# Row-wise inverse norms by VectorE transposes, with new orders on four engines, in a two-layer graph kernel

## The reference

```python
# layer 0: y = x mixed over the nodes with adj * adj, plus bias
x = layernorm(x + einsum('bnf,nm->bmf', x, adj * adj) + bias)
# layer 1, h = x
z_l, z_g, v = h @ W_lang.T, h @ W_grav.T, h @ W_V.T
zn  = z_l / max(norm(z_l), EPS)
A_l = max(zn @ zn.T, 0) * not_eye
d2  = max(sq + sq.T - 2 * z_g @ z_g.T, 0)          # sq = sum(z_g * z_g)
A_g = exp(-d2 / (2 * sigma**2)) * not_eye
K_l = A_l * adj / max(rowsum(A_l * adj), EPS)       # K_g likewise
K   = sigmoid(gate) * K_l + (1 - sigmoid(gate)) * K_g
x = layernorm(h + (K @ v) @ W_O.T)
```

## Time and profile before

| | us |
|---|---|
| median of 3 runs | 592.41 (591.02 to 592.76) |
| the profiled execution | 591.92 |
| its span | 590.1 |
| TensorE busy | 574.5 (97% of the span) |
| VectorE busy | 437.9 (74%) |
| ScalarE busy | 296.8 (50%) |
| GpSimd busy | 140.5 (24%) |
| mean granted TensorE clock, as a share of full speed | 0.994 |

### The profile page before, as it was taken

The page is one execution under the profiler, slowest core; times in us unless marked ns, Lnnn a source line. Parts: engine busy times, 40 slices in busy tenths (PEclk is TensorE's granted clock), DMA queues, the critical chain, the costliest instruction groups (busy, mean ns, idle before and its releaser), DMA issues.

```text
span 590.1 us, 10012 instructions
## 1 busy us (share of the span) xinstructions
PE 574.5 (97%) x3681; PEld 445.5 (75%) x3681; DVE 437.9 (74%) x1022; ACT 296.8 (50%) x516; POOL 140.5 (24%) x344
## 2 busy tenths in 40 slices
PE   8999999999999999999999999999999999999991
PEld 6887868687786868688686868778686868868770
DVE  4934796859689695959779586968968595977586
ACT  4644427365462636456372746546263644637323
POOL 0202103132321304132320313232130413222022
PEclk9999999999999999999999999999999999999997
DMA  8813030321313031131304022131304110100003
GB/s 287 203 31 71 1 72 19 84 60 54 72 72 72 24 112 29 53 90 56 72 37 107 19 83 61 54 72 72 72 19 113 32 55 18 54 1 37 37 0 142
DMA packets 20783, 38.67 MB, mean 66 GB/s; under 512 B 2176, under 2 KB 2176, under 8 KB 20736
## 3 DMA queue, kind: packets, MB, share of 16 engines
q1 hardware_dynamic: 20736, 38.05, 22.8%
HBM read 21.27 MB, written 16.78 MB: 64 GB/s over the span
## 4 chain that ended last, share of the span: by engine, by line
PE 93%; DVE 4%; issue 1%; DMA 1%; ACT 0%; POOL 0%; SPq 0%; POOLq 0%; DVEq 0%
PE ring L388 63%; PE bank_s L407 10%; PE bank_z L361 3%; PE bank_y L348 3%; PE bank_y L361 2%; PE bank_z L439 2%; PE bank_s L348 2%; PE bank_y L439 2%; PE ring L490 2%; PE ring L513 1%; DVE KT L880 1%; DVE z_bn L891 1%; DMA yT<-in_L_gnn_W_lang_dram 1%; DVE P_turned L815 1%; PE bank_y L419 1%
## 5 line engine op out<-in xcount | busy, mean ns | idle before, releaser
L576 ACT ACTIVATE yT<-ring 128x512 f32<-128x512 f32 x128 | 72.6, 593 | 138.0 <-PE ring L388 138.0
L388 PE MATMUL ring<-hT_hi,T_hi 128*128 128x512 f32 x320 | 127.5, 399 | 0.0
L388 PE MATMUL ring<-hT_hi,T_lo 128*128 128x512 f32 x320 | 124.8, 390 | 0.0
L388 PE MATMUL ring<-hT_lo,T_hi 128*128 128x512 f32 x288 | 112.4, 390 | 0.0
L388 PE MATMUL ring<-M_hi,hT_hi 128*128 128x512 f32 x256 | 102.7, 401 | 0.0
L388 PE MATMUL ring<-M_hi,hT_lo 128*128 128x512 f32 x256 | 100.2, 392 | 0.0
L388 PE MATMUL ring<-M_lo,hT_hi 128*128 128x512 f32 x256 | 99.7, 390 | 0.0
L780 DVE TENSOR_TENSOR hT_lo<-hT,hT_hi 128x512 fp32r<-128x512 f32 x64 | 42.3, 681 | 76.2 <-ACT hT L576 76.1
L388 PEld LDWEIGHTS ring<-hT_hi,T_hi 128*128 128x128 f32 x320 | 60.1, 188 | 23.9 <-issue 12.2
L585 ACT ACTIVATE h_sb<-h_sb,y_nb,y_rs 128x512 f32<-128x512 f32 x64 | 52.1, 815 | 50.1 <-POOL y_nb L1086 50.1
L1081 POOL TENSOR_SCALAR y_ve<-y_mv 128x2 f32<-128x2 f32 x32 | 7.6, 237 | 264.9 <-DVE y_mv L774 263.6
(11 more groups left out here) (135 smaller groups left out, 820.9 us busy)
## 6 DMA issues: line engine op xcount, KB each, us to landing
x_sb<-in_x_dram SPq DMA_DIRECT2D x32, 512.0 KB, 6.4
out_dram<-h_sb SPq DMA_DIRECT2D x60, 256.0 KB, 2.0
yT<-in_L_gnn_W_lang_dram SPq DMA_DIRECT2D x4, 256.0 KB, 3.2
yT<-in_L_gnn_W_grav_dram SPq DMA_DIRECT2D x1, 1024.0 KB, 7.6
h_sb<-in_L_gnn_W_V_dram SPq DMA_DIRECT2D x1, 1024.0 KB, 11.3
h_sb<-in_L_gnn_W_O_dram SPq DMA_DIRECT2D x1, 1024.0 KB, 12.7
out_dram<-h_sb SPq DMA_DIRECT2D x8, 128.0 KB, 2.4
bias_bc<-in_L_gnn_bias_dram SPq DMA_DIRECT2D x1, 256.0 KB, 8.4
```

The costliest lines, as they stand in the source:

```text
L388: last = pe.matmul(ring[ring_of(g, k)][:, :], a, b, start=n == 0, stop=n == len(terms) - 1)
L576: return act.activation(dst, src, ACT.Copy, scale=scale)
```

## The change

The transposes of `inv_rep` leave TensorE. GpSimd spreads each inverse norm over 32 columns in place of 64, VectorE turns the 32x32 blocks with eight transposes into `inv_row` in SBUF, and `weigh` is one instruction over 128 partitions that reads SBUF only, in place of four over 64 partitions that read PSUM. With `row_ps` gone from bank_y0, the waits that protected it go too; GpSimd waits for the transposes of the group before, since it overwrites `inv_rep`. AT_Y is 5 in place of 4, and the lists of TensorE, ScalarE, VectorE and GpSimd are rewritten, for the step and for group 15.

```diff
-    AT_Y = 4
+    AT_Y = 5
-        inv_rep = sb("inv_rep", [R, NP, N])
+        inv_rep = sb("inv_rep", [R, NP, N // 2])
+        inv_row = sb("inv_row", [R, NP, N])
...
@@ TensorE: layer0, apply_k lose the waits for x0_done; rows(g) is gone
-            def rows(g):
-                pe.wait_ge(inv_ready, g + 1)
...
-                for h in range(2):
-                    last = pe.transpose(row_ps[:, h, :], inv_rep[:, 2 * h:2 * h + 2, :].rearrange("r a j -> r (a j)"),
-                                        ident[:, :])
-                last.then_inc(rows_done, 1)
...
             def step(g, tail=True):
                 project(g, 0)
+                layer0(g + 1, 0)
                 project(g, 1)
                 project(g, 2)
                 project(g, 3)
-                layer0(g + 1, 0)
+                project(g, 4)
                 if tail:
                     apply_k(g - 1, 0)
+                    apply_k(g - 1, 1)
                 layer0(g + 1, 1)
-                if tail:
-                    apply_k(g - 1, 1)
-                project(g, 4)
                 project(g, 5)
                 project(g, 6)
                 project(g, 7)
...
                 gram(g)
+                project(g, 9)
                 transpose_h(g + 1, 2)
-                project(g, 9)
+                transpose_h(g + 1, 3)
                 project(g, 10)
-                transpose_h(g + 1, 3)
                 project(g, 11)
-                rows(g)
...
@@ TensorE, group 15
             project(g, 5)
+            apply_k(g - 1, 0)
             project(g, 6)
             project(g, 7)
-            apply_k(g - 1, 0)
+            apply_k(g - 1, 1)
             gram(g)
-            apply_k(g - 1, 1)
             project(g, 8)
-            rows(g)
...
@@ ScalarE, group 15
             copy_p(g)
+            normalise_out(g - 1, 0)
             exp_g(g)
             evict(g, 8)
             evict(g, 9)
-            evict(g, 10)
-            normalise_out(g - 1, 0)
-            evict(g, 11)
             normalise_out(g - 1, 1)
             normalise_out(g - 1, 2)
+            evict(g, 10)
             normalise_out(g - 1, 3)
+            evict(g, 11)
...
@@ VectorE
+            def rows(g):
+
+                dve.wait_ge(inv_ready, g + 1)
+                B = N // 2
+                for b in range(2):
+                    for i in range(2):
+                        for j in range(2):
+                            row, col = b * N + i * B, b * N + j * B
+                            last = dve.transpose(inv_row[row:row + B, :, j * B:(j + 1) * B], inv_rep[col:col + B, :, :])
+                last.then_inc(rows_done, 1)
...
-                for a in range(2):
-                    for c in range(2):
-                        last = dve.scalar_tensor_tensor(X0[half(a), :, c, :], S2[half(a), :, L, c, :], 0.0,
-                                                        row_ps[half(c), :, half(a)], ALU.max, ALU.mult)
+                last = dve.scalar_tensor_tensor(X0[:, :, :, :], S2[:, :, L, :, :], 0.0,
+                                                inv_row[:, :, :].rearrange("r (h a) j -> r h a j", a=2), ALU.max, ALU.mult)
...
             def step(g, tail=True):
                 add_y(g + 1, 0)
                 add_y(g + 1, 1)
+                double_lo(g)
+                count_y(g + 1, 0)
                 if tail:
                     add_z(g - 1, 0)
...
                 lo_hT(g + 1, 0)
                 diagonals(g)
-                lo_hT(g + 1, 1)
                 shift(g)
                 if tail:
-                    count_z(g - 1, 3)
+                    gather_z(g - 1, 1)
                 turn_p(g)
-                if tail:
-                    gather_z(g - 1, 1)
+                lo_hT(g + 1, 1)
                 lo_hT(g + 1, 2)
                 lo_hT(g + 1, 3)
+                rows(g)
                 add_p(g)
                 weigh(g)
...
@@ GpSimd, columns(g)
+                if g > 0:
+                    pool.wait_ge(rows_done, g)
-                pool.tensor_copy(inv_rep[:, :, :], inv_norm[:, :].unsqueeze(2).broadcast_to([R, NP, N])).then_inc(
+                pool.tensor_copy(inv_rep[:, :, :], inv_norm[:, :].unsqueeze(2).broadcast_to([R, NP, N // 2])).then_inc(
```

More of the change, by code:

```diff
@@ L343, in layer0 @@
                     pe.wait_ge(hT_copied, NP * g - 2)
-                    if g > 1:
-                        pe.wait_ge(x0_done, g - 1)
                 for c in range(2):
@@ L428, in apply_k @@
                     pe.wait_ge(z_added, NP * g)
-                    pe.wait_ge(x0_done, g + 1)
                 elif h and g < NG - 2:
@@ L434, in apply_k @@
                     pe.wait_ge(hT_copied, NP * g + 2 * NP)
-                    if h:
-                        pe.wait_ge(x0_done, g + 1)
                 for c in range(2):
@@ L625, in step @@
                 evict(g, 4)
+                normalise_h(g + 1, 0)
                 evict(g, 5)
-                normalise_h(g + 1, 0)
                 evict(g, 6)
@@ L630, in step @@
                 evict(g, 7)
-                evict(g, 8)
-                normalise_h(g + 1, 2)
-                if tail:
-                    normalise_out(g - 1, 0)
                 hi_hT(g + 1, 0)
@@ L637, in step @@
                 copy_p(g)
+                normalise_h(g + 1, 2)
+                normalise_h(g + 1, 3)
                 copy_hT(g + 1, 1)
                 hi_hT(g + 1, 1)
-                normalise_h(g + 1, 3)
+                if tail:
+                    normalise_out(g - 1, 0)
+                copy_hT(g + 1, 2)
+                evict(g, 8)
+                hi_hT(g + 1, 2)
                 evict(g, 9)
-                copy_hT(g + 1, 2)
-                hi_hT(g + 1, 2)
+                copy_hT(g + 1, 3)
+                hi_hT(g + 1, 3)
                 evict(g, 10)
-                hi_hT(g + 1, 3)
-                copy_hT(g + 1, 3)
                 if tail:
                     normalise_out(g - 1, 1)
+                    normalise_out(g - 1, 2)
+                evict(g, 11)
+                if tail:
+                    normalise_out(g - 1, 3)
                 exp_g(g)
-                if tail:
-                    normalise_out(g - 1, 2)
-                    normalise_out(g - 1, 3)
-                evict(g, 11)
             def hi_weight(i, c):
@@ L905, in step @@
                 add_y(g + 1, 1)
+                double_lo(g)
+                count_y(g + 1, 0)
                 if tail:
                     add_z(g - 1, 0)
+                add_y(g + 1, 2)
+                add_y(g + 1, 3)
+                if tail:
                     count_z(g - 1, 0)
-                add_y(g + 1, 2)
-                if tail:
                     add_z(g - 1, 1)
                     count_z(g - 1, 1)
+                    add_z(g - 1, 2)
+                    count_z(g - 1, 2)
                     gather_z(g - 1, 0)
[L914 to L918, removed]
                     add_z(g - 1, 3)
                 count_y(g + 1, 1)
-                double_lo(g)
                 if tail:
-                    count_z(g - 1, 2)
+                    count_z(g - 1, 3)
                 lo_hT(g + 1, 0)
                 diagonals(g)
-                lo_hT(g + 1, 1)
                 shift(g)
                 if tail:
-                    count_z(g - 1, 3)
+                    gather_z(g - 1, 1)
                 turn_p(g)
-                if tail:
-                    gather_z(g - 1, 1)
+                lo_hT(g + 1, 1)
                 lo_hT(g + 1, 2)
                 lo_hT(g + 1, 3)
+                rows(g)
                 add_p(g)
@@ L1037, in _ @@
             g = NG - 1
+            add_z(g - 1, 0)
             double_lo(g)
-            add_z(g - 1, 0)
             count_z(g - 1, 0)
@@ L1042, in _ @@
             count_z(g - 1, 1)
+            add_z(g - 1, 2)
+            count_z(g - 1, 2)
+            gather_z(g - 1, 0)
+            add_z(g - 1, 3)
+            count_z(g - 1, 3)
             diagonals(g)
+            gather_z(g - 1, 1)
             shift(g)
-            add_z(g - 1, 2)
             turn_p(g)
+            rows(g)
             add_p(g)
@@ L1049, in _ @@
             coefficients(g)
-            gather_z(g - 1, 0)
-            add_z(g - 1, 3)
             combine(g)
             turn_k(g)
-            count_z(g - 1, 2)
-            count_z(g - 1, 3)
             add_z(g, 0)
-            gather_z(g - 1, 1)
+            add_z(g, 1)
             count_z(g, 0)
-            add_z(g, 1)
+            add_z(g, 2)
             count_z(g, 1)
-            add_z(g, 2)
+            add_z(g, 3)
             gather_z(g, 0)
-            add_z(g, 3)
             count_z(g, 2)
@@ L1112, in step @@
                 scale_y(g + 1, 0)
+                scale_y(g + 1, 1)
                 if tail:
                     scale_z(g - 1, 0)
-                scale_y(g + 1, 1)
                 columns(g)
```

6 lines of the change are left out of this document (removed).

## The result

The changed kernel takes 595.86 us (median of 5 runs, 595.11 to 596.25) where the kernel before takes 591.50 (5 runs): ratio 1.0067, 95% interval 1.0053 to 1.0081. By the ratio it is slower by about 4.0 us (3.1 to 4.8); the two medians lie 4.4 apart. The forecast was 597.6 us, 5.7 us slower.

What follows compares the result with a forecast made beforehand. TensorE's instruction stream was taken to bound groups 0 to 14, the road from gram through VectorE to KT the last group; +3.8 and +1.9 us made +5.7, on 591.92 us: 597.6 us, own range 594.3 to 600.5, overall 592.2 to 600.8.

Steps and rivals of the forecast that it cites:

- TensorE's stream sets the time: Groups 0 to 14: TensorE is busy for all of its 33.80 us; other engines matter only if they become late.
- A second block, +0.37 us: TensorE, each group: layer 0 half 0 standing apart makes two blocks of 64x64 tiles, adding one fixed price, 0.37 us.
- The pair, -0.23 us: TensorE, each group: the two transposes of inv_rep between projections leave, removing 0.23 us of path.
- The h transposes, +0.11 us: TensorE around the gram: projection 9 follows it, t2 and t3 come together before 10; +0.11 us, bounds -0.06 and +0.36.
- Per group: TensorE, groups 0 to 14: 0.37 - 0.23 + 0.11 = +0.25 us, bounds +0.08 and +0.50; in all +3.8 us.
- VectorE's work is hidden: Gram to KT: VectorE's road grows 1.4 us, but apply_k half 0 comes later, leaving 1.6 us to spare.
- ScalarE's list: Ring evictions: ScalarE evicts in time, its longest detour fitting into 2.7 us of projection 9 and transposes; priced at nothing.
- The last group, +1.9 us: Group 15: gram ends 1.23 us later, gram to KT +0.65, z work behind 0.0; +1.9 us, bounds 1.2 and 2.6.
- Free switches: Rival, TensorE: layer 0 half 0 standing alone pays no block price, only the pair's removal counts; 590.0 us, chance 0.10.
- Half-price switches: Rival, TensorE: switches cost half, near 0.18 us, h transposes gain 0.05, tail +1.5; about 592.4 to 593 us, chance 0.09.
- KT's road overtaking Ka: Rival, every group: the longer road to KT ends after apply_k half 0 is due; 604.6 us, chance 0.05.
- Projection 7: Rival, ring: projection 7 is caught waiting for its bank, 14 x 0.3 = +4 us, 601.8 us, chance 0.04.

Runs made afterwards that it cites:

- La alone moved: Kernel before, with only the layer 0 pass for half 0 (La) moved behind projection 0: 598.17 us, ratio 1.0097.
- The first experiment: Kernel before, with inverse norms turned by VectorE and one product, all other orders and AT_Y as before: 629.36 us, ratio 1.0637.
- the kernel with the old order: Kernel before, with inverse norms by VectorE, old orders, and eviction 11 before exp_g on ScalarE: 613.11 us, ratio 1.0366.

## Why the prediction was right, step by step

**TensorE's stream sets the time.** Right. Both traces show it busy for the whole group, and every change of a group's distance (34.14, 34.19, 33.55 us) came back in the time.

**A second block, +0.37 us.** Right: +0.35 in the trace, +0.39 with La alone moved. The price was read from a block of four passes and isolated ones in the last group, and held in another place between other neighbours. The Trainium skill says in TensorEngine Tiling (Array Packing), section Key Properties, that changing the tiling mode drains TensorE. The fixed part agrees with it in kind; no run separates a drain from whatever else a change of tiles costs.

**The pair, -0.23 us.** Right: 0.23 of path before, 0.28 when put back.

**The h transposes, +0.11 us.** The term that was mis-sized, with bounds that held it. The gram's exit of 0.10 was as chosen (0.11). Eight transposes in a row I took at 0.96, between my two bounds of 0.81 and 1.05, which is also what t0 and t1 take in front of the gram; in front of a projection they take 0.79 + 0.08 = 0.87. The gram, its exit and all four transposes come to 5.61 against 5.57, so +0.04. The same eight take 0.96 in front of the gram and 0.79 in front of a projection; the 0.17 between them would fit a switch into the gram's tiles, which no run isolates.

**Per group** therefore +0.16, not +0.25, and 15 x 0.16 = 2.4 us, not 3.8. This is most of the difference between 5.7 and 4.0. Between the first projections of group 0 and of group 15 the two traces differ by 2.2 us.

**VectorE's work is hidden.** Right in the changed kernel: 1.86 us to spare, 1.6 said, since the road grew by 1.13 us and not by 1.4. But the list of roads was incomplete. The first experiment lost its time on the road from S through exp_g and eviction 11 to the ring, where I had priced ScalarE's list at nothing after looking only at the evictions beside the gram. The changed kernel avoids it by its order; the term was right there without having been worked out, which is luck, and in another order it would have been a large miss.

**The last group, +1.9 us.** The gram comes 1.23 us later as worked out. From gram's start to KT done it was 19.22 us before and is 19.81 after:

```profile
560.75 3.71 PE L405 MATMUL bank_s<-yT,hT 128*64 128x128 f32 x64
...
578.04 2.52 DVE L869 STREAM_TRANSPOSE KT<-K_sb 32x128 f32<-32x128 f32 x8
```

That is +0.59 where I had +0.65 (my terms add up to 0.63). Behind Ka it is 0.13 us shorter. In all +1.7. What was wrong there is projection 11: it was to end 2 to 3 us before KT, and TensorE was to wait as long; it ended about 1 us before, because its matmuls ran at a lower clock behind the wait. It cost nothing, but with only 0.95 us to spare.

**The sum.** 2.4 + 1.7 = 4.1 us, and 4.0 were measured. The profiled executions differ by 3.2 us only (595.11 and 591.92). The one after, the fastest of its five, reached the first projection 0.93 us earlier, at 38.21 in place of 39.14. From there to the end it is 551.0 us before and 554.9 after: +3.9. The early start does not come from the change: two of the experiments whose setup is that of the changed kernel reach the first projection at 39.42 and 39.00. What makes the setup vary is open. The prediction states two ranges, 594.3 to 600.5 and 592.2 to 600.8; both hold the 595.86.

**The rivals.** Free switches (590.0) fell with La moved alone. Half-price switches fell likewise. KT's road overtaking Ka exists in the kernel with the old order, at about 1.5 us a group. Projection 7 never waited in the changed kernel.

## What to carry to other kernels

Where TensorE's stream is full, count the visits to another tile shape, not only the matmuls: here each extra visit cost as much as one and a half of the pairs whose removal was the point. Before lengthening a road on an engine with spare time, list every road that leaves it, those through a third engine's queue and a shared ring too, since work in order makes one late instruction hold all behind it. And a wait whose end nobody needs may be harmless or even useful: here its removal only moved the idle time to a place where the lower clock behind it cost 0.9 us.

## What the runs showed of the hardware

TensorE's clock was not expected. After 5.05 us and 5.3 us of idle time before Ka in group 15, Ka's first pass took 1.76 us in place of 0.91, at a granted clock of 0.50. In the changed kernel, behind a wait of 2.2 us at projection 11, the matmuls stood 0.43 us apart in place of 0.23 for about 3.4 us:

```profile
575.80 0.63 PE L386 MATMUL ring<-M_hi,hT_lo 128*128 128x512 f32 x1
576.23 0.63 PE L386 MATMUL ring<-M_hi,hT_hi 128*128 128x512 f32 x1
```

```profile
575.40:578.80 3.40, 3.40 (x10) 2.66 (x9) 3.00 (x9) 2.67 (x5) 0.00 (x0) 0.50 0.40 154
```

Behind a short wait the outcome is not fixed by the place or by the length of the wait. Before Ka of group 15 TensorE idles 2.4 us in the kernel before and in the one with La moved alone, at the same place of the same list. In the first trace Ka and Kb then ran at full speed. In the second the clock fell while Ka ran:

```profile
577.49 1.09 PE L439 MATMUL bank_z<-u_sb,KT 64*64 64x512 f32 x8 [2.37 <-DVE KT L880]
578.40 1.04 PE L439 MATMUL bank_y<-u_sb,KT 64*64 64x512 f32 x8
```

```profile
583.25 1.63 PE L439 MATMUL bank_z<-u_sb,KT 64*64 64x512 f32 x8 [2.36 <-DVE KT L880]
584.64 1.95 PE L439 MATMUL bank_y<-u_sb,KT 64*64 64x512 f32 x8
```

The granted clock of Kb there:

```profile
584.64:586.40 1.76, 1.76 (x12) 0.27 (x4) 1.47 (x5) 0.00 (x0) 0.39 (x2) 0.50 0.00 0
```

From Ka's start to the end it took 0.5 us longer for that. The first experiment shows the same among its groups: fourteen waits of nearly the same length, and the lower clock behind five of them. What decides it was not found.

It also bears on the times of the kernel before. Of its 43 executions beside the experiments that ran at the usual clock, 16 have a mean granted clock of 0.994 or 0.995 and take 591.5 us on average; the other 27 have 0.990 to 0.992 and take 592.5. The profiled one is of the first kind. A slow Ka in the last group would explain the second kind, but no execution of that kind was profiled. So a difference of 1 us between two of these kernels can be the clock of the last group, and is best read from the first projection to the end in traces that show that clock.
